# Matmuls that nobody reads, added to the tensor engine's program at both ends of an attention pipeline

## The chip, the cores and the metric

The kernel runs on one core of one Trainium2 chip. The metric is the device time of one execution in microseconds (us), from start to end. A "granted clock" of 1.00 in the profile means TensorE at 2.4 GHz, 0.50 means 1.2 GHz; a figure between them is the mean over a stretch in which both occurred.

## The reference: what is computed

The input is x of 8 x 512 rows of 512 numbers. Three residual blocks follow each other, each on the layer-normalised rows:

```python
x = x + 0.5 * ffn(layernorm(x))     # 16 experts choose 256 rows each; one shared 512x512 matrix
x = x + attention(layernorm(x))     # below
x = x + 0.5 * ffn(layernorm(x))
```

```python
q, k, v = x @ Wq, x @ Wk, x @ Wv                  # 16 heads, 4 shared k/v heads, q and k twice 32 wide
energy  = causal(rope(q) . rope(k))               # two maps for each head
scores  = softmax(energy / sqrt(32))
diff    = softmax(causal(scores[0] - lam * scores[1]))
att     = rmsnorm(diff @ v) @ Wo
```

## The kernel before

The program has three blocks. The first computes the expert layer, whose choice of rows is a search with small steps. The second, called the attention stage here, computes attention and, for each tile, the router logits and the expert product of the last block. The third makes the second choice and adds.

**Tiles.** The 4096 rows are 32 tiles of 128. Each matrix product with a weight is split into fp16 high and low parts (`three`, lines 229 to 235): 3 matmuls for each of 4 slices of the contraction, so 12 matmuls of 512 columns for a 512-wide result.

**The attention stage.** Every engine runs the same schedule, `run_bodies`. There are 33 bodies, K = 0 to 32, each of 8 steps (a step is one head for two of the four row tiles), each step of three slots; slot 3j+i is slot i of step j. On TensorE a step has the energies (`energies`, L1928 and L1930), the fp32 transposes of the difference (`turn_diff`, L1942), and the product with v (`weigh`, L1960, fp32, 33 columns). Beside these, a body does side work, given by a table from slot to functions:

- `prep(f)` works on tile tau = K + 5, the one that is to be projected: turn x (slot 1), three projections (slots 5, 7, 13), three groups of transposes (12, 19, 22). From K = 27 on there is no such tile, tau is `None`, and these slots are empty. PSUM bank 4 belongs to this work.
- `post(f)` works on tile pi = K - 5, the one that is to be finished: turn the heads (slot 7), the product with Wo (`product_o`, 10), turn x2 (17), route (20), expert (21). For K = 0 to 4 pi is `None`. PSUM bank 5 belongs to this work.

So bodies 0 to 4 have projections and nothing to finish (called the head bodies here), bodies 5 to 26 have both (the middle), bodies 27 to 31 only finish (the tail), and body 32 drains the steps that lag behind; its side table ends at slot 12. Before body 0 a prologue prepares tiles 0 to 4; after body 32 a closing finishes the last tiles. TensorE issues in program order, so whatever stands in a slot is done before the matmuls of the next slot. `energies(1)` waits until ScalarE has read the bank of the step before (`exp_done`); the bank 6 of the transposes is shared, and each use waits for ScalarE's `probs` (L1692).

**The order of the last block.** Nothing of the second choice starts before the closing has ended.

Of the kernel before, what the change touches and what calls it, by code (L numbers as in the profile page):

```python
# [31 lines left out]
KT = E // P  # L32
# [152 lines left out]
def program(nc, x, wqkv, wo, we, wr, lams, rms, rb, eb, consts, out, x1_d, x2_d, y2_d):  # L185
# [14 lines left out]
    with top:  # L200
# [709 lines left out]
        with ExitStack() as ctx:  # L910
# [994 lines left out]
            def _(pe):  # L1905
# [2 lines left out]
                    s.start(pe)  # L1908


                def energies(i):
                    def f(at):
                        j = at.j
# [51 lines left out]
                def prep(f):  # L1965
                    return lambda tau, pi: f(tau) if tau is not None else None

                def post(f):
                    return lambda tau, pi: f(pi) if pi is not None else None
# [84 lines left out]
                    tr.then_inc(rt_done.sem, 1)  # L2054

                def prologue():
                    first_turn(0)
                    for u in range(AHEAD):
                        first_project(u, 0)
                        if u >= 1:  # L2060
                            first_chunks(u - 1, 1)
                        first_project(u, 1)
                        if u >= 1:
                            first_chunks(u - 1, 2)
                        if u + 1 < AHEAD:
                            first_turn(u + 1)
                        first_project(u, 2)
                        first_chunks(u, 0)
                    first_chunks(AHEAD - 1, 1)
                    first_chunks(AHEAD - 1, 2)  # L2070
# [30 lines left out]
                def close_heads(q):  # L2101
                    al_done.wait(pe, LAST + q)
                    if q >= 2:
                        at_out.wait(pe, LAST + q - 2)
                    close_turn(c_pair(0, q), c_split(q), ant_done)
# [23 lines left out]
                def closing():  # L2129
# [2 lines left out]
                    expert(LAST - 1)  # L2132
                    prob_done.wait(pe, 2 * pair(NT - 1, STEPS - 1) + 1)
                    att_out.wait(pe, (NT // TB) * H - 1)
                    close_heads(0)
                    close_o(0)
                    close_heads(1)
# [13 lines left out]

                run_bodies(pe, [[(0, energies(1)), (0, energies(0)), (7, turn_diff(1))], [(8, weigh), (6, turn_diff(0))],
                                []],
                           {1: [prep(turn_x)], 5: [prep(project(0))], 7: [post(turn_heads), prep(project(1))],
                            10: [post(product_o)], 12: [prep(turn_chunks(0))], 13: [prep(project(2))],
                            17: [post(turn_x2)], 19: [prep(turn_chunks(1))], 20: [post(route)], 21: [post(expert)],
                            22: [prep(turn_chunks(2))]}, {},
                           prologue,
                           closing)
# [102 lines left out]
```

## Time and profile before

| | |
|---|---|
| time, median of 3 runs | 1826.18 us (1823.63 to 1830.19) |
| the profiled execution: its own time, its span | 1838.54 us, 1836.7 us |
| mean granted TensorE clock | 0.863 |
| busy share: TensorE, VectorE, ScalarE, GpSimdE | 80%, 79%, 69%, 59% |
| the attention stage's bodies with energies | from 288.0 us to 1663.2 us |

The span is the time from the first to the last instruction. A busy share is over the whole span and mixes stages. Matmuls are pipelined, so the duration of one is longer than the distance to the next; where a cost is worked out, the distance between two starts is used. The start of a body is taken as the start of its first energy matmul (L1928; 32 a body).

### The profile page before, as it was taken

Reading aid. Unit: us, or ns where it says so; the run is one execution under the profiler, and the core shown is the slowest. Engines: PE = TensorE matmul, PEld = TensorE weight load, DVE = VectorE, ACT = ScalarE, POOL = GpSimd, SP = SyncE. Lnnn points to the kernel's source line nnn. Section 1 sums busy time; section 2 is a strip of 40 time slices with the busy share of each in tenths; the row PEclk is TensorE's granted clock in tenths of the full one; section 3 lists DMA queues with packets and bytes.
Section 4 is the critical chain, followed back from the end, with each engine's and each line's share of the span. In section 5 each row is a group of like instructions: output and inputs, shape, how many; then the busy total and the mean of one; then the engine's idle time right before and its main releaser. Section 6 shows DMA issues by size and latency. Waiting matters only on the chain. (4 is left out here: it accounts for less than half of the span.)

```text
span 1836.7 us, 43825 instructions
## 1 busy us (share of the span) xinstructions
PE 1473.0 (80%) x10688; PEld 1035.1 (56%) x10688; DVE 1456.8 (79%) x5505; ACT 1260.1 (69%) x3426; POOL 1082.6 (59%) x1493
## 2 busy tenths in 40 slices
PE   3997645888898998889888898888988888888620
PEld 3543322666666666666666666666666666666310
DVE  5778425888889898898889988898989877674477
ACT  2363334888788888888888888888888876675320
POOL 4421443666677677776777777777777665554300
PEclk9998776788899899999999899998999887676855
DMA  8023321111111111121111111121211100001186
GB/s 304 2 64 135 118 66 42 29 32 36 32 46 46 44 50 50 44 50 44 44 44 44 44 44 50 46 52 45 51 46 45 42 19 21 19 17 41 41 312 252
DMA packets 179673, 117.30 MB, mean 64 GB/s; under 512 B 139169, under 2 KB 139553, under 8 KB 179618
## 3 DMA queue, kind: packets, MB, share of 16 engines
q1 hardware_dynamic: 179618, 116.65, 21.5%
q8 instruction: 25, 0.41, 0.1%
q14 instruction: 30, 0.25, 0.0%
HBM read 51.57 MB, written 33.55 MB: 46 GB/s over the span
## 5 line engine op out<-in xcount | busy, mean ns | idle before, releaser
L1675 ACT ACTIVATE ex<-bank,nbias 128x512 f32<-128x512 f32 (+3 forms) x1024 | 527.7, 538 | 83.2 <-DVE bank L1220 80.6
L1220 DVE TENSOR_SCALAR_CACHE_REDUCE bank<-bank,nesc 128x512 f32<-128x512 f32 (+3 forms) x1024 | 503.3, 551 | 84.6 <-PE bank L1930 83.9
L1960 PEld LDWEIGHTS bank<-vs,pr 128*128 128x128 f32 x2560 | 336.3, 207 | 24.5 <-issue 12.7
L1960 PE MATMUL bank<-vs,pr 128*128 (+1 forms) x2560 | 341.4, 284 | 9.8 <-DVE att L1266 5.3
L1942 PE MATMUL bank<-cst,df 128*128 128x128 f32 x1280 | 265.9, 310 | 83.6 <-ACT pr L1692 83.0
L1928 PE MATMUL bank<-ks,qs 96*128 (+2 forms) x1024 | 266.2, 337 | 68.7 <-ACT ex L1675 45.4
L1522 POOL TENSOR_SCALAR ex<-ex,gam 128x128 f32<-128x128 f32 (+3 forms) x512 | 317.3, 630 | 0.0
L1692 ACT ACTIVATE pr<-bank 128x128 f32<-128x128 f32 (+3 forms) x512 | 231.7, 453 | 88.5 <-PE bank L1942 87.3
L1246 DVE CUSTOM_DVE_ANT_0 df<-ex 128x128 f32<-128x128 f32 (+3 forms) x512 | 261.1, 525 | 8.2 <-issue 3.7
L1942 PEld LDWEIGHTS bank<-cst,df 128*128 128x128 f32 x1280 | 169.8, 167 | 111.0 <-ACT pr L1692 96.2
L1675 ACT ACTIVATION_READ_ACCUMULATOR ex<-bank,nbias 128x1 f32 x1024 | 222.6, 217 | 0.0
L1930 PE MATMUL bank<-mask_b,ident_b 128*128 128x128 bf16 x1024 | 210.2, 239 | 0.0
L1684 ACT ACTIVATE df<-df,dbias,rsum 128x512 f32<-128x512 f32 (+1 forms) x256 | 201.7, 788 | 0.0
L1928 PEld LDWEIGHTS bank<-ks,qs 96*128 (+1 forms) x1024 | 110.8, 108 | 160.7 <-issue 96.1
L1529 POOL TENSOR_SCALAR df<-df,rsum,dbias 128x128 f32<-128x128 f32 (+1 forms) x256 | 147.1, 575 | 40.9 <-DVE dbias L1255 40.8
L1605 POOL TENSOR_TENSOR split<-rot,split 128x512 f16<-128x512 f32 (+1 forms) x81 | 80.4, 993 | 111.3 <-ACT split L1720 111.3
L232 PE MATMUL bank<-wqkv_h,b_xt 128*128 128x512 f16 x360 | 142.3, 395 | 3.2 <-ACT turned L1762 1.2
L234 PE MATMUL bank<-wqkv_h,b_xt 128*128 128x512 f16 x360 | 142.9, 397 | 0.0
L233 PE MATMUL bank<-wqkv_l,b_xt 128*128 128x512 f16 x360 | 142.2, 395 | 0.0
L1234 DVE SCALAR_TENSOR_TENSOR gam<-esum,lam,rsum 128x2 f32<-128x2 f32 x256 | 114.8, 449 | 33.7 <-DVE rsum L1227 24.5
L1220 DVE DVE_READ_ACCUMULATOR bank<-bank,nesc 128x1 f32 x1024 | 141.2, 138 | 0.0
L1515 POOL TENSOR_SCALAR_AFFINE_SELECT ex<-ex 128x256 f32<-128x256 f32 x256 | 120.9, 472 | 22.2 <-DVE gam L1234 22.2
(359 smaller groups left out, 2954.5 us busy)
## 6 DMA issues: line engine op xcount, KB each, us to landing
qs<-turned SPq DMA_DIRECT2D x360, 64.0 KB, 2.1
x_dram<-xa SPq DMA_DIRECT2D x8, 1024.0 KB, 4.9
c_x<-x_dram SPq DMA_DIRECT2D x8, 1024.0 KB, 14.7
c_y<-y_dram SPq DMA_DIRECT2D x8, 1024.0 KB, 14.7
out_dram<-c_x SPq DMA_DIRECT2D x8, 1024.0 KB, 4.7
b_xs<-x_dram SPq DMA_DIRECT2D x30, 256.0 KB, 2.7
xa<-in_x SPq DMA_DIRECT2D x7, 1024.0 KB, 13.6
x<-x_dram SPq DMA_DIRECT2D x28, 256.0 KB, 2.6
```

The lines of the kernel that those rows point to most:

```text
L234: mm = eng.matmul(acc, a_lo(k), b_hi(k), start=False, stop=last and k == KT - 1)
L1220: dve.tensor_scalar(part, part, nesc[:, 0:1], None, ALU.mult, ALU.min, accum_out=nbias[:, j, i, a:a + 1]).then_inc(bias_done.sem, 1)
L1246: dve.tensor_tensor_reduce(out=df[j % 4][:, lo:hi], in0=ex[j % 4][:, 0, lo:hi], in1=ex[j % 4][:, 1, lo:hi], scale=1.0, scalar=-3e38, op0=A ...
L1522: gp.tensor_scalar(ex[j % 4][:, 1, lo:hi], ex[j % 4][:, 1, lo:hi], gam[:, j, i:i + 1], 1.0, ALU.mult, ALU.mult).then_inc(scaled.sem, 1)
L1529: gp.tensor_scalar(df[j % 4][:, lo:hi], df[j % 4][:, lo:hi], rsum[:, j, 0, 0:1], dbias[:, j, 0:1], ALU.mult, ALU.add).then_inc(shifted_sho ...
L1675: ac.activation(ex[j % 4][:, a, lo:hi], energy(j, i)[:, a, :], ACT.Exp, bias=nbias[:, j, i, a:a + 1], scale=-1.0, accum_out=esum[:, j, i, ...
L1684: ac.activation(df[j % 4][:, lo:hi], df[j % 4][:, lo:hi], ACT.Identity, bias=dbias[:, j, 1:2], scale=rsum[:, j, 1, 0:1]).then_inc(shifted_ ...
L1692: ac.activation(pr[j % 2][:, lo:hi], bank[:, 6, 0:hi - lo], ACT.Exp).then_inc(prob_done.sem, 1)
L1928: pe.matmul(out_e, q.rearrange("p a n -> p (a n)"), k.rearrange("p a n -> p (a n)"), start=True, stop=True)
L1930: mm = pe.matmul(out_e[:, n - P:n], ident_b[:, :], mask_b[:, :], start=False, stop=True, skip_group_check=True)
L1942: tr = pe.transpose(bank[:, 6, k * P:(k + 1) * P], df[j % 4][:, lo + k * P:lo + (k + 1) * P], ident)
L1960: mm = pe.matmul(bank[:, 7, t * DV:(t + 1) * DV], pr[j % 2][:, lo + k * P:lo + (k + 1) * P], val, start=(k == 0), stop=(k == t))
```

## The change

A helper `busy(n, at)` issues n matmuls of 128 x 128 weights (the fp16 identity) and 512 fp16 columns (a slice of the expert matrix) into PSUM bank `at`. Nobody reads the result, and no semaphore is raised. `idle_prep(n)` calls it in bodies in which tau is `None`, into bank 4; `idle_post(n)` in bodies in which pi is `None`, into bank 5. Twelve more are put ahead of the first transposes of the prologue, behind a new wait for the first normalised tile (`xn_done`), and twelve into the closing, between the last waits and `close_heads(0)`.

Counted: 28 in each of the bodies 27 to 31 (slots 2, 5, 7, 10, 13, 18 and 21, four each), 16 in body 32 (slots 2, 5, 7, 10), 12 in each of the bodies 0 to 4 (slots 11, 16, 20), 12 in the prologue, 12 in the closing: 240 in all.

```diff
+                def busy(n, at):
+
+                    for i in range(n):
+                        pe.matmul(bank[:, at, :], ident_h[:, :], we_h[:, i % KT, :], start=True, stop=True)
+
+                def idle_prep(n):
+                    return lambda tau, pi: busy(n, 4) if tau is None else None
+
+                def idle_post(n):
+                    return lambda tau, pi: busy(n, 5) if pi is None else None
...
                 def prologue():
+                    xn_done.wait(pe, 0)
+                    busy(12, 0)
                     first_turn(0)
...
                     att_out.wait(pe, (NT // TB) * H - 1)
+                    busy(12, 4)
                     close_heads(0)
...
-                           {1: [prep(turn_x)], 5: [prep(project(0))], 7: [post(turn_heads), prep(project(1))],
-                            10: [post(product_o)], 12: [prep(turn_chunks(0))], 13: [prep(project(2))],
-                            17: [post(turn_x2)], 19: [prep(turn_chunks(1))], 20: [post(route)], 21: [post(expert)],
+                           {1: [prep(turn_x)], 2: [idle_prep(4)], 5: [idle_prep(4), prep(project(0))], 7: [idle_prep(4), post(turn_heads), prep(project(1))],
+                            10: [idle_prep(4), post(product_o)], 12: [prep(turn_chunks(0))], 11: [idle_post(4)], 13: [idle_prep(4), prep(project(2))],
+                            16: [idle_post(4)], 17: [post(turn_x2)], 19: [prep(turn_chunks(1))], 18: [idle_prep(4)], 20: [idle_post(4), post(route)], 21: [idle_prep(4), post(expert)],
                             22: [prep(turn_chunks(2))]}, {},
```

## Rows read from the trace of the kernel before

**Rows 1.** The page, busy tenths and granted clock in 40 slices of the span.

```profile
PE   3997645888898998889888898888988888888620
DVE  5778425888889898898889988898989877674477
PEclk9998776788899899999999899998999887676855
```

**Rows 2.** Busy time by stretch, bodies 6 to 8; columns: stretch, length, engines, clock, DMA.

```profile
535.59:577.07 41.48, 36.85 (x305) 26.89 (x303) 38.86 (x154) 35.89 (x102) 31.24 (x44) 1.00 0.19 49
577.07:623.10 46.03, 41.28 (x305) 29.09 (x302) 39.71 (x154) 36.78 (x103) 34.62 (x51) 0.89 0.17 44
623.10:665.64 42.54, 38.05 (x305) 27.92 (x302) 39.13 (x154) 36.38 (x102) 30.55 (x42) 0.96 0.18 48
```

**Rows 3.** The same view, the five tail bodies, K = 27 to 31.

```profile
1453.83:1494.29 40.46, 35.18 (x241) 27.48 (x239) 31.15 (x134) 31.87 (x94) 24.52 (x37) 0.79 0.18 45
1494.29:1535.11 40.82, 35.08 (x240) 27.44 (x238) 31.47 (x134) 31.54 (x93) 24.49 (x37) 0.79 0.06 19
1535.11:1581.71 46.60, 41.22 (x239) 30.58 (x237) 31.28 (x134) 31.88 (x93) 24.61 (x37) 0.67 0.05 17
1581.71:1626.24 44.53, 39.91 (x240) 30.18 (x238) 31.26 (x134) 31.66 (x93) 24.53 (x37) 0.69 0.06 18
1626.24:1663.16 36.92, 32.12 (x208) 25.29 (x206) 28.66 (x120) 27.75 (x83) 21.47 (x32) 0.72 0.06 21
```

**Rows 4.** The same view, head bodies K = 0, 1 and 3.

```profile
288.01:324.67 36.66, 24.83 (x135) 13.69 (x136) 28.68 (x116) 23.80 (x75) 17.67 (x26) 0.69 0.16 35
324.67:366.49 41.82, 37.99 (x248) 29.12 (x249) 33.93 (x144) 33.12 (x99) 26.09 (x42) 0.79 0.14 32
407.91:449.10 41.19, 34.98 (x248) 26.00 (x249) 34.14 (x145) 33.11 (x99) 25.94 (x41) 0.88 0.13 30
```

**Rows 5.** The same view, short stretches in body 29, in the drain and before the closing.

```profile
1531.60:1545.10 13.50, 10.45 (x81) 7.54 (x78) 8.98 (x41) 10.79 (x34) 7.04 (x8) 1.00 0.05 19
1545.20:1558.60 13.40, 13.38 (x56) 9.25 (x57) 7.73 (x33) 8.26 (x24) 9.28 (x15) 0.50 0.00 0
1671.40:1688.50 17.10, 14.62 (x63) 10.52 (x62) 5.16 (x17) 6.15 (x11) 8.92 (x9) 0.50 0.08 26
1695.30:1712.30 17.00, 8.42 (x43) 4.38 (x43) 7.26 (x18) 4.33 (x7) 13.39 (x5) 0.50 0.00 1
```

**Rows 6.** TensorE's instructions in order of time, body 28 and 29; columns: start, duration.

```profile
1532.10 0.38 PE L233 MATMUL bank<-we_l,at 128*128 128x512 f16 x1
1532.31 0.38 PE L234 MATMUL bank<-we_h,at 128*128 128x512 f16 x1
...
1553.88 0.63 PE L233 MATMUL bank<-wo_l,at 128*128 128x512 f16 x1
1554.30 0.63 PE L234 MATMUL bank<-wo_h,at 128*128 128x512 f16 x1
...
1558.57 0.48 PE L1928 MATMUL bank<-ks,qs 96*128 x1
```

**Rows 7.** TensorE's waits in the tail bodies : total us, times, longest; the largest.

```profile
PE bank L1928 <- ACT ex L1675: 21.9, 16, 2.3
```

**Rows 8.** Order of time at the prologue: VectorE, TensorE, and SyncE's stacking DMAs.

```profile
196.17 0.55 DVE L1306 TENSOR_SCALAR b_xs<-b_xs,norms 128x512 f32<-128x512 f32 x1 [0.67 <-POOL norms L1551]
...
198.71 1.03 PE L2027 MATMUL bank<-ident_h,att 128*128 128x128 f16 x8 [25.39 <-POOL att L1555]
...
200.85 0.61 PE L232 MATMUL bank<-wqkv_h,b_xt 128*128 128x512 f16 x1 [1.10 <-ACT b_xt L1777]
...
219.24 8.41 SPq L1123 DMA_DIRECT2D qs<-turned  x12
```

**Rows 9.** TensorE in order of time at the closing.

```profile
1712.08 0.75 PE L2098 MATMUL bank<-ident_h,qs 128*128 128x128 f16 x8
1713.94 0.39 PE L232 MATMUL bank<-wo_h,qs 128*128 128x512 f16 x1 [1.10 <-ACT qs L1853]
```

## The prediction

> **What bounds the kernel now.** I read the page's slices first, then the busy times cut at the starts of bodies, then order of time and waits where the clock moves. In the page the reader is to see two dips of the granted clock that lie inside the attention stage: the head bodies and, deeper, the tail (the digits 7, 6, 7, 6 of the clock under an 8 or 9 of TensorE) [rows 1]. The last dip, to 5, is the second choice, which runs on VectorE; the change does not touch it.
>
> In the middle three engines are close: at full clock body 6 takes 41.48 us with TensorE busy 36.85 and VectorE 38.86, that is 89% and 94% [rows 2]. There the clock alone changes the length: 42.54 us at 0.96, 46.03 at 0.89. A clock of c over a body of length l holds 2(1 - c)l of time at 1.2 GHz, called cold time below. For body 7 that is 10.1 us, and it is 4.55 us longer than body 6: 0.45 us for each cold us.
>
> The tail is where one sees something odd [rows 3]. VectorE has 31 us of work a body instead of 39, ScalarE 32 instead of 36, TensorE some 240 matmuls instead of 305, and yet the bodies take 40.5 to 46.6 us. TensorE is the engine that fills them, 87% to 90% busy, because it is slow: the clocks of 0.79, 0.79, 0.67, 0.69 and 0.72 are 17.0, 17.1, 30.8, 27.6 and 20.7 us of cold time, 113 of 209.3 us. From body 28 to 29 the length rises by 5.78 us for 13.7 cold us: 0.42. I take 0.43 us for each cold us.
>
> What precedes a fall or a rise? In body 29 the clock is full for 13.5 us, in which TensorE is busy 10.45, falls after that, and stays at 1.2 GHz for 13.4 us in which it is busy 13.38 [rows 5]. So busy time by itself does not bring the clock back. It comes back behind the twelve 512-column matmuls of the product with Wo: those start 0.43 us apart, and the energies at 1558.57 already speed up [rows 6]. At full clock they start 0.21 to 0.22 us apart. Dense 512-column matmuls are the ingredient that the tail has lost with its projections (36 of them a body), and are what the change adds (28 a body).
>
> The Trainium skill (TensorE: Matmul & The Clock Gate, Part 1) says that sustained activity releases the throttle and that idle gaps bring it back. Taken literally it speaks against the change: TensorE is busy throughout the cold stretch [rows 5], so more matmuls would add only their own time. The same page, Part 4, says that transposes do not count as busy in the same way; the tail's steps consist largely of fp32 transposes and of 33-column products, and with that the trace agrees.
>
> **The change, term by term.** *Tail, bodies 27 to 31.* First, what a warm tail would be without additions: 40.46 - 17.0 x 0.43 = 33.1, and likewise 33.5, 33.4 and 32.7 us for the next three, which agree, and 28.0 for the shorter last one. At 33.2 us VectorE's 31.3 would be 94%, the share it reaches in body 6, so this is also a floor.
>
> Now the additions: 28 x 0.216 = 6.0 us of TensorE a body. Its busy time of 35.18 us shrinks by half of the cold time to 26.7, and grows to 32.7. At the 89% that TensorE reaches in body 6, a body takes 36.8 us at full clock. That is dearer than 33.2: in this form the additions hide only partly. What can hide them is TensorE's wait for ScalarE before the energies, 21.9 us in 16 places of the five bodies, none over 2.3 us [rows 7]; the groups of four (0.86 us) stand mostly right before energies. Those in slots 10 and 21 stand ahead of a product or an expert, where TensorE is behind anyway, and are exposed. At 1.2 GHz a group costs 1.7 us and nothing hides it.
>
> How much cold time remains is the disputed number. The middle, whose 36 dense matmuls come in three lumps, has 0, 10.1 and 3.4 us in its three bodies [rows 2], 4.5 on average; the additions are spread over seven places and ought to do as well. I take 4.5 us, 1.9 us of length. The four bodies are then 38.7 us each. Body 31, with 24 of the additions ahead of its last energies, is (32.12 - 10.3 + 5.2) / 0.89 + 1.9 = 32.2. Sum 187.0 against 209.3: **-22.3 us**. Bounds: full clock throughout, 177.5, so -31.8; the clock of today throughout, which is a rival below.
>
> *Drain, body 32.* Cold from 1671.4 to 1688.5 [rows 5]. Its end would be 7.4 us earlier without that; I take half, 3.7, and half of the 16 x 0.216 = 3.5 us exposed: **-2.0**, between -7 and +5.
>
> *Closing.* The twelve come where TensorE follows the expert's product without a pause, and ScalarE waits for the transposes behind them (1.10 us from its copy back to TensorE) [rows 9]. The clock is up from 1712.3 on, before it has work there, so nothing is gained: 12 x 0.216 = **+2.6**; at 1.2 GHz it would be 5.1. No cover: the last block waits for the closing's end.
>
> *Prologue.* The added wait ends with the first normalised tile, at 196.7; TensorE then would have waited until 198.71 for the low part [rows 8]. Twelve cold matmuls end at 201.8, 3.1 us late. In exchange the clock rises earlier, and about six of the first projection's matmuls, today at 0.43 us, cost 0.21 less each: **+1.8**, between 0 and 3.1. Everything behind follows, since SyncE's queue of stacking DMAs starts from that projection's results at 219.24 and is what body 0 waits for.
>
> *Head, bodies 0 to 4.* Here length hardly follows the clock: body 1 has 17.6 cold us and 41.82 us, body 3 has 9.9 and 41.19 [rows 4], 0.08 per cold us. So little is to be won, and 12 x 0.216 = 2.6 us find 6.2 us of idle TensorE in body 3. Nothing for bodies 1 to 4, **-1** for the start in body 0 (22.7 cold us); between -4 and +6. The middle is unchanged but meets the clock in another phase: 0, plus or minus 3.
>
> Sum: -22.3 - 2.0 + 2.6 + 1.8 - 1 = -20.9, from 1838.5 to 1817.6 for the profiled execution. The median of the timed runs is 12.4 us lower than that. Bodies 29 and 30 together are 9.9 us longer than 27 and 28 for the same work; if that is what the timed executions lack, only 11 us are to be won there. I go halfway: -16 from 1826.2, **1810 us**.
>
> **Rivals.** *The clock stays* (slower). If the additions do not change when it falls and rises, the 136 in the five bodies cost about 0.33 us each at today's mix, 45 us, of which the 21.9 us of waits can swallow half their own length or all of it: +23 to +34; with drain +5, closing +2.6 and prologue +3.1 the time is about 1860 to 1871. For it: the long busy cold stretch, and that a group of four is a third of what stood before the rise in body 29. Against it: the middle, where as dense a mixture holds 0.89 to 1.00. *The point from which this decides*: exposed additions are between 136 x 0.216 - 16 x 0.86 = 15.6 and 29.4 us at full clock, so the cold time must fall by 36 to 68 of 113 us, that is, the tail's clock must reach 0.82 to 0.89. *Bought even*: the clock reaches about 0.85, gain and price cancel, and only closing and prologue remain: 1822 to 1832. *Slower by the head*: the same place in the projections' chain (slot 11 ahead of the transposes of chunk 0) could delay rope and stacking by up to its 0.86 us a body, +6 at most with the others; this alone moves the result but does not turn it.
>
> **How the numbers follow.** The tail clocks over 0.89: 0.60, giving 1793 to 1819. Bought even: 0.17. The clock stays or rises little, and the time is above 1832: 0.23. A measurement of this kernel tells 0.3%, 5.5 us, from no change; so faster 0.62, same 0.15, slower 0.23. Low end: the full-clock tail against the timed median, 1826.2 - 31.8 + 2.6 + 1.8 - 1 = 1797.8, and some 4 for the drain: 1794. High end: into the slower rival, whose mild form, a clock of 0.80, gives some +10: 1836. The likeliest case alone spans 1794 to 1820.
>
> **What would show it.** Right: tail clocks of 0.9 and more, bodies of 37 to 40 us, TensorE still near 88% busy, waits for ScalarE before energies fewer than 16; head bodies still 41 to 42 us; close_heads 2.6 us later behind the expert, the first projection 2 us later. Wrong: tail clocks near 0.8 with bodies of 43 us or more; or full clocks and bodies of 40 us, which would mean that the 6 us are exposed on top of VectorE's floor, not beside it.

## The result and the profile after

In the session of the recorded result the changed kernel is slower, by under one per cent: median 1843.56 us (19 runs, 1829.54 to 1852.55) against 1826.77 us of the kernel before (19 runs, 1823.31 to 1854.24). The ratio is 1.0075, with a 95% interval of 1.005 to 1.01. The forecast was 1810 us and "faster"; the time lies above the range's 1836. The profiled execution took 1848.64 us, with a span of 1846.8 us. Ratios and intervals here and below leave out the few runs that lie more than 1.5% above the fastest of their kernel; medians and counts keep them.

The times of the changed kernel fall into two groups: over all sessions of this study none of its 31 runs lies between 1837.3 and 1843.4 us, 19 lie below (median 1833.2) and 12 above (1849.2), and 11 of those 12 belong to the 19 runs of the first session. The kernel before has no such gap. Its 94 runs crowd at 1822 to 1830 and thin out up to 1860; cut at the same 1840, a line drawn after the fact, 70 lie below (1826.7) and 24 above (1849.3). So two things have to be explained: some 6.5 us, or 0.36%, between the lower groups, and how often a run lies far above.

The slices of the page, kernel after, of 46 us each. They answer to [rows 1]:

```profile
PE   3996735999999989898998888999998988887720
...
PEclk9998877778899998999999999999999899998865
```

The dip of the tail (7, 6, 7, 6 before) has become 9, 9, 9, 8: the clock did what the change is made for. The digits of the head are what they were, and that is the first disappointment.

The windows between the first energies of successive bodies, kernel after: start and end, length, then the busy time and count of TensorE, its weight loads, VectorE, ScalarE and GpSimd, the granted clock, the DMA share and GB/s. The order is bodies 0, 1, 3 and 4, a body of the middle, all of bodies 5 to 26, the tail's bodies 27 to 31, and from the last energies to the closing transposes. They answer to [rows 2 to 4]:

```profile
286.11:320.76 34.65, 23.57 (x147) 12.84 (x148) 28.59 (x116) 23.81 (x75) 17.68 (x26) 0.84 0.17 37
320.76:364.81 44.05, 40.18 (x260) 28.98 (x261) 33.94 (x144) 33.12 (x99) 26.09 (x42) 0.81 0.13 30
...
408.99:453.25 44.26, 40.39 (x261) 29.05 (x261) 33.91 (x145) 33.12 (x99) 26.01 (x41) 0.81 0.13 28
453.25:494.26 41.01, 37.15 (x260) 27.14 (x261) 34.13 (x145) 33.13 (x99) 25.95 (x41) 0.88 0.14 30
...
984.90:1029.28 44.38, 39.78 (x305) 28.09 (x303) 38.92 (x154) 36.38 (x102) 31.96 (x45) 0.92 0.18 46
...
494.26:1473.54 979.28, 881.00 (x6623) 624.73 (x6624) 855.51 (x3368) 800.58 (x2246) 706.87 (x995) 0.92 0.18 45
...
1473.54:1515.18 41.64, 37.20 (x268) 26.54 (x266) 31.08 (x134) 31.98 (x94) 24.59 (x37) 0.92 0.18 44
1515.18:1554.40 39.22, 34.11 (x268) 24.20 (x266) 31.32 (x134) 31.45 (x93) 24.59 (x37) 1.00 0.06 20
1554.40:1594.38 39.98, 35.38 (x268) 25.01 (x266) 31.36 (x134) 31.55 (x93) 24.51 (x37) 0.96 0.06 20
1594.38:1634.84 40.46, 36.55 (x268) 26.13 (x266) 31.22 (x134) 31.56 (x93) 24.21 (x37) 0.92 0.06 19
1634.84:1668.44 33.60, 28.51 (x233) 20.58 (x230) 28.71 (x121) 27.55 (x83) 22.22 (x33) 1.00 0.07 23
...
1668.44:1722.37 53.93, 40.47 (x232) 27.84 (x231) 19.52 (x63) 19.67 (x41) 26.55 (x21) 0.75 0.09 30
```

The same windows of the kernel before that [rows 2 to 4] don't have, all of bodies 5 to 26 and the stretch behind the last energies:

```profile
490.20:1453.83 963.63, 864.80 (x6622) 623.76 (x6623) 862.28 (x3368) 800.75 (x2246) 712.64 (x995) 0.93 0.18 46
...
1663.16:1712.08 48.92, 35.81 (x199) 25.38 (x198) 19.61 (x65) 19.66 (x41) 27.18 (x22) 0.65 0.10 33
```

Span against span, 1836.7 to 1846.8, the 10.1 us are made up like this:

| stretch | before | after | difference |
|---|---|---|---|
| start to first energies | 288.0 | 286.1 | -1.9 |
| body 0 | 36.7 | 34.7 | -2.0 |
| bodies 1 to 4 | 165.5 | 173.5 | +8.0 |
| bodies 5 to 26, not touched | 963.6 | 979.3 | +15.7 |
| bodies 27 to 31 | 209.3 | 194.9 | -14.4 |
| last energies to closing transposes | 48.9 | 53.9 | +5.0 |
| the rest | 124.6 | 124.4 | -0.2 |

The largest term is in bodies in which nothing was added: there nearly every body takes 44.4 us, where before their average was 963.6 / 22 = 43.8.

In the waits of TensorE over bodies 27 to 31, kernel after (total us, times, longest), the first row answers to [rows 7]:

```profile
PE bank L1939 <- ACT ex L1675: 13.5, 17, 1.4
...
PE bank L1953 <- ACT pr L1692: 5.0, 14, 0.6
```

The waits before the energies, 21.9 us in 16 places before, became 13.5 us in 17. The second row is a wait for ScalarE at the transposes of the difference; the kernel before had 1.5 us of it in 5 places. So the waits for ScalarE shrank by about 5 us in all, and the additions are 29.4 us of matmuls (136 x 0.216).

The order of time on TensorE at both ends, kernel after (start, duration, line, tiles, and in brackets the wait before it); it answers to [rows 8, 9]:

```profile
193.96 4.45 PE L1914 MATMUL bank<-we_h,ident_h 128*128 128x512 f16 x12 [23.45 <-DVE b_xs L1306]
198.24 0.61 PE L2038 MATMUL bank<-ident_h,att 128*128 128x128 f16 x8
199.96 0.39 PE L232 MATMUL bank<-wqkv_h,b_xt 128*128 128x512 f16 x1 [1.10 <-ACT b_xt L1777]
...
1719.77 2.75 PE L1914 MATMUL bank<-we_h,ident_h 128*128 128x512 f16 x12
1722.37 0.61 PE L2111 MATMUL bank<-ident_h,qs 128*128 128x128 f16 x8
```

Behind the expert the twelve take 2.60 us from their start to that of the closing transposes.

### The profile page after: what moved, and what is told of

It is laid out like the page before. It is cut to its first block and busy times, and to the rows that moved or that the text cites. A ratio compares the mean times of both kernels' runs of the same rounds, so it can differ in the third digit from the quotient of the medians.

```text
span 1846.8 us, 44305 instructions
## 1 busy us (share of the span) xinstructions
PE 1495.6 (81%) x10928; PEld 1025.7 (56%) x10928; DVE 1448.8 (78%) x5505; ACT 1259.3 (68%) x3426; POOL 1076.8 (58%) x1493
## 5 line engine op out<-in xcount | busy, mean ns | idle before, releaser
L1971 PEld LDWEIGHTS bank<-vs,pr 128*128 128x128 f32 x2560 | 322.2, 199 | 26.8 <-issue 14.4
L1971 PE MATMUL bank<-vs,pr 128*128 (+1 forms) x2560 | 326.9, 278 | 12.3 <-DVE att L1266 7.4
L1953 PE MATMUL bank<-cst,df 128*128 128x128 f32 x1280 | 257.4, 303 | 88.3 <-ACT pr L1692 87.6
L1522 POOL TENSOR_SCALAR ex<-ex,gam 128x128 f32<-128x128 f32 (+3 forms) x512 | 313.5, 623 | 0.0
L1939 PE MATMUL bank<-ks,qs 96*128 (+2 forms) x1024 | 254.6, 325 | 52.9 <-ACT ex L1675 29.7
L1246 DVE CUSTOM_DVE_ANT_0 df<-ex 128x128 f32<-128x128 f32 (+3 forms) x512 | 256.6, 516 | 9.2 <-issue 4.7
L1675 ACT ACTIVATION_READ_ACCUMULATOR ex<-bank,nbias 128x1 f32 x1024 | 227.9, 223 | 0.0
L1953 PEld LDWEIGHTS bank<-cst,df 128*128 128x128 f32 x1280 | 162.5, 161 | 116.5 <-ACT pr L1692 102.4
L1941 PE MATMUL bank<-mask_b,ident_b 128*128 128x128 bf16 x1024 | 203.1, 233 | 0.0
L1684 ACT ACTIVATE df<-df,dbias,rsum 128x512 f32<-128x512 f32 (+1 forms) x256 | 202.4, 791 | 0.0
L232 PE MATMUL bank<-wqkv_h,b_xt 128*128 128x512 f16 x360 | 138.9, 386 | 3.2 <-ACT turned L1762 1.2
L234 PE MATMUL bank<-wqkv_h,b_xt 128*128 128x512 f16 x360 | 138.1, 384 | 0.0
```

What stands on the lines that cost most here:

```text
L232: eng.matmul(acc, a_hi(k), b_hi(k), start=first and k == 0, stop=False)
L1246: dve.tensor_tensor_reduce(out=df[j % 4][:, lo:hi], in0=ex[j % 4][:, 0, lo:hi], in1=ex[j % 4][:, 1, lo:hi], scale=1.0, scalar=-3e38, op0=A ...
L1522: gp.tensor_scalar(ex[j % 4][:, 1, lo:hi], ex[j % 4][:, 1, lo:hi], gam[:, j, i:i + 1], 1.0, ALU.mult, ALU.mult).then_inc(scaled.sem, 1)
L1675: ac.activation(ex[j % 4][:, a, lo:hi], energy(j, i)[:, a, :], ACT.Exp, bias=nbias[:, j, i, a:a + 1], scale=-1.0, accum_out=esum[:, j, i, ...
L1684: ac.activation(df[j % 4][:, lo:hi], df[j % 4][:, lo:hi], ACT.Identity, bias=dbias[:, j, 1:2], scale=rsum[:, j, 1, 0:1]).then_inc(shifted_ ...
L1939: pe.matmul(out_e, q.rearrange("p a n -> p (a n)"), k.rearrange("p a n -> p (a n)"), start=True, stop=True)
```

## The experiments

Every kernel below computes all that the reference asks for; where an edit is called "nothing of the change", the additions are other ones than the change's. Each was timed in five rounds, beside the kernel before on the same chip. Lengths of bodies are windows as above, from one profiled execution of each kernel. Each diff is against the kernel that it varies: the changed kernel for the three parts, tail_only for tail_lean, the kernel before for middle_fill, middle_fill for middle_three, and middle_three for middle_thin and combined. The sessions' medians of the kernel before are 1829.32 (first four experiments, 35 runs), 1832.75 (next four, 23) and 1834.57 (last four, 17).

### The change in three parts

**tail_only**, the additions in bodies 27 to 31 alone.

```diff
 def idle_prep(n):
-    return lambda tau, pi: busy(n, 4) if tau is None else None
+    return lambda tau, pi: busy(n, 4) if tau is None and not isinstance(pi, int) else None
...
 def prologue():
-    xn_done.wait(pe, 0)
-    busy(12, 0)
...
-    busy(12, 4)
     close_heads(0)
...
-    ... 11: [idle_post(4)], ... 16: [idle_post(4)], ... 20: [idle_post(4), post(route)] ...
+    ... 20: [post(route)] ...
```

> Only the 28 added matmuls in each of the bodies 27 to 31; nothing in the head, the prologue, the drain, the closing. Theory A (the tail's additions pay, the loss lies elsewhere): the tail takes 195 us instead of 209, as in the changed kernel; the timed runs that leave the middle at 43.7 us a body are 4 to 14 us faster than those of before. Theory B (the tail's additions cost what they bring): no gain, and any tail shorter than 209 us in the profile is already given back in the drain.

Measured: median 1823.65 us (12 runs, 1819.22 to 1840.24), ratio 0.9977, interval 0.994 to 1.0013. The tail takes 197.0 us. Two of its windows:

```profile
1451.40:1490.64 39.24, 34.26 (x267) 24.24 (x266) 31.17 (x134) 31.76 (x94) 24.60 (x37) 1.00 0.18 47
1490.64:1533.10 42.46, 39.38 (x266) 28.41 (x265) 31.32 (x134) 32.07 (x93) 24.22 (x37) 0.84 0.05 19
```

Alternate bodies hold the full clock all through, as the theory wants, and even those are no shorter than 39.2 us. Where the clock falls for part of a body, it takes 42.5. The middle takes 960.1 us, as it does in ends_only, tail_double and tail_half: tail additions alone do not disturb it. (The 963.6 us of the kernel before come mostly from its last middle body, 44.1 us instead of 40.9.)

**head_only**, the additions of slots 11, 16 and 20 in bodies 0 to 4 alone (slots 2, 5, 7, 10, 13, 18 and 21 and both ends taken out).

```diff
-    2: [idle_prep(4)], 5: [idle_prep(4), prep(project(0))], ...
+    5: [prep(project(0))], 7: [post(turn_heads), prep(project(1))], 10: [post(product_o)], 11: [idle_post(4)], ...
```

> Only the 12 added matmuls in each of the bodies 0 to 4. Theory A: they slow bodies 1 to 3 from 41.4 to 44.2 us as in the changed kernel, 8 us, of which body 0 gives back 2; the time is 5 to 8 us above before. Rival (those long head bodies were a chance meeting of schedule and clock, not the additions' price): head bodies of 41 to 42 us, no change beyond 3 us.

Measured: median 1833.83 us (12 runs, 1829.53 to 1852.68), ratio 1.0037, interval 1.0002 to 1.0073. Body 0, body 2, body 3, and the first part of body 2 and of body 3:

```profile
289.06:324.20 35.14, 24.06 (x148) 12.96 (x148) 28.61 (x116) 23.82 (x75) 17.68 (x26) 0.84 0.17 37
...
368.56:412.81 44.25, 40.39 (x260) 29.06 (x261) 33.86 (x144) 33.05 (x99) 25.95 (x41) 0.81 0.12 28
412.81:453.81 41.00, 37.13 (x261) 27.10 (x261) 34.15 (x145) 33.13 (x99) 25.95 (x41) 0.88 0.13 30
...
368.56:382.20 13.64, 13.64 (x63) 10.19 (x64) 8.14 (x37) 9.84 (x29) 8.72 (x15) 0.50 0.29 61
...
412.90:419.70 6.80, 6.80 (x39) 5.58 (x40) 5.05 (x22) 5.86 (x17) 6.22 (x11) 0.50 0.26 56
```

Body 2 begins with 13.64 us at a clock of 0.50, that is at 1.2 GHz throughout, with TensorE busy for all of it; body 3 does so for 6.80 us. That is the difference between 44.25 and 41.00 us. Where the cold stretch is short, the additions are free: 41.0 is what such a body took before [rows 4]. Body 0 gains some 1.5 us. The head costs more than it gives.

The additions do not themselves stand in the cold stretch. In body 2 they start at 390.42, 401.87 and 406.15 us, and the granted clock around each is 1.00; from 368.56 to 382.20 TensorE runs only what the kernel before has there too. And the long cold stretch is not theirs alone. Of seven profiles in which bodies 1 to 4 have no additions, six show four bodies of 41.1 to 41.9 us, and one, that of tail_lean below, shows 39.7 us and then three of 44.2 to 44.4. The three profiles with additions there show three, two and two bodies of 44.0 to 44.4 us.

**ends_only**, the twelve ahead of the first turn and the twelve ahead of close_heads alone (all of the slots' additions taken out).

```diff
-    2: [idle_prep(4)], 5: [idle_prep(4), prep(project(0))], ... 11: [idle_post(4)], ...
+    5: [prep(project(0))], 7: [post(turn_heads), prep(project(1))], ...
```

> Only the twelve matmuls in the prologue and the twelve in the closing. Theory A: closing +2.6 us, prologue 0 to +2, nothing gained: +2 to +5 us, and the middle may fall into its other pattern (44.37 us a body instead of 43.69), which would add 14 us more in some runs. Rival (the prologue's additions warm the clock for what follows): body 0 shorter by 2 us or more and no loss in all.

Measured: median 1831.81 us (12 runs, 1824.72 to 1850.88), ratio 1.003, interval 0.9985 to 1.0075. Its tail has no additions, so it is also a second look at the tail of the kernel before, the first four bodies:

```profile
1447.38:1487.93 40.55, 34.98 (x239) 27.47 (x238) 31.12 (x134) 31.87 (x94) 24.51 (x37) 0.79 0.17 45
1487.93:1528.78 40.85, 34.88 (x239) 27.43 (x238) 31.46 (x134) 31.54 (x93) 24.49 (x37) 0.79 0.05 19
1528.78:1570.26 41.48, 35.44 (x239) 27.77 (x238) 31.45 (x134) 31.77 (x93) 24.56 (x37) 0.79 0.06 19
1570.26:1610.80 40.54, 34.78 (x239) 27.41 (x238) 31.27 (x134) 31.55 (x93) 24.50 (x37) 0.79 0.06 19
```

None is like bodies 29 and 30 of [rows 3], with 46.60 and 44.53 us at 0.67 and 0.69. The tail takes 198.5 us (198.2 in head_only, 199.4 in middle_fill, 198.7 on average), not 209.3. A good 10 us of what there was to win was a mishap of the one profiled execution.

Below 1840 us the medians of the three parts are 1822.85, 1833.5 and 1830.15, against 1826.7 of the kernel before: -3.9, +6.8 and +3.4. They sum to +6.3, and the lower group of the changed kernel lies +6.5 higher. That they agree to 0.2 us is luck: against the runs of the kernel before in their own session (1825.7) the parts are -2.8, +7.9 and +4.5, in sum +9.5, and each rests on 8 to 11 runs that spread over 9 to 19 us. What holds is the order: the tail gains 3 to 4 us, the head loses 7 to 8, the ends 3 to 5.

### What the tail's bodies are bound by

**tail_lean**, tail alone, 20 a body instead of 28: none in slots 2, 10 and 21, eight in slot 13.

```diff
-    2: [idle_prep(4)], ... 10: [idle_prep(4), post(product_o)], ... 13: [idle_prep(4), prep(project(2))], ... 21: [idle_prep(4), post(expert)]
+    10: [post(product_o)], ... 13: [idle_prep(8), prep(project(2))], ... 21: [post(expert)]
```

> Only the tail, 20 added matmuls a body instead of 28, at the places behind which the clock fell in the tail without additions (slots 5, 7, 13, 18; eight in slot 13, where TensorE still waited 1.4 us with four); nothing in slots 2, 10 and 21. If the price of an addition is its own time wherever TensorE does not wait, the three dropped groups give back up to 2.6 us a body: 37 to 38 us at full clock instead of 39.2, 8 to 12 us in all against before. If the length of a warm tail body is not set by TensorE, it stays 39 us and the time stays that of the tail alone.

Measured: median 1811.22 us (6 runs, 1806.02 to 1836.27), ratio 0.9888, interval 0.9827 to 0.995. The profiled execution is the longest of the six, 1836.27 us, so its lengths are not those of a typical run. Its tail takes 190.4 us; two of its windows:

```profile
1470.57:1508.69 38.12, 35.17 (x259) 25.80 (x258) 31.00 (x134) 31.57 (x94) 24.62 (x37) 0.91 0.19 48
...
1589.16:1627.43 38.27, 33.82 (x258) 24.28 (x257) 31.39 (x134) 31.59 (x93) 24.58 (x37) 0.96 0.07 21
```

At a clock of 0.91 such a body is shorter than one with 28 additions at full clock (39.24 in tail_only). So some of the groups in slots 2, 10 and 21 are paid for; which ones is shown step by step below.

Where the excess of this execution lies can be read too. Bodies 1 to 4 and bodies 5 to 26, none of which this kernel changes:

```profile
325.49:498.08 172.59, 147.58 (x993) 107.81 (x994) 135.92 (x573) 132.45 (x390) 104.35 (x162) 0.84 0.13 29
498.08:1470.57 972.49, 872.27 (x6600) 628.01 (x6623) 860.23 (x3368) 802.31 (x2246) 714.86 (x995) 0.92 0.18 46
```

They are 7 and 12 us longer than the usual 165.5 and 960.1. Long executions thus exist without any addition outside the tail, and the head has a part in them.

**tail_double**, tail alone, every group 8 instead of 4, so 56 a body (`idle_prep(8)` in each of the seven slots).

> Only the tail, groups of eight instead of four (56 a body). If additions are paid in full at full clock: 39.2 + 6.0 = 45.2 us a body and +25 us or more against the tail alone. If they are half hidden, as my prediction had it: 42 us and +13 us.

Measured: median 1828.37 us (12 runs, 1823.69 to 1850.27), ratio 1.0005, interval 0.9963 to 1.0046. The tail takes 200.3 us. A body at full clock:

```profile
1492.08:1533.16 41.08, 39.18 (x295) 26.92 (x293) 31.24 (x134) 31.41 (x93) 24.21 (x37) 1.00 0.06 19
```

28 more additions are 28 x 0.216 = 6.0 us of matmuls; the body grows from 39.2 to 41.1 us. Two thirds went into time in which TensorE would have waited. So at 39.2 us TensorE was not the bound, and at 41.1, busy 39.18, it nearly is.

**tail_half**, tail alone, groups of 2, so 14 a body (`idle_prep(2)` in each of the seven slots).

> Only the tail, groups of two in all seven slots (14 a body). With 28 a body a full-clock body took 39.2 us, with 56 it took 41.1: 1.9 us for 6.0 us of matmuls. If that line goes on, a full-clock body with 14 takes 38.3 us; if an unadded warm body is as short as my prediction had it (33.2 us), it takes 36 us. With only 14 the clock will fall once or twice a body, so the tail as a whole takes 194 to 200 us.

Measured: median 1832.86 us (12 runs, 1826.43 to 1850.56), ratio 1.0001, interval 0.9961 to 1.0041. The tail takes 202.4 us, some 4 more than with none. The worst body:

```profile
1489.39:1533.44 44.05, 39.71 (x253) 29.48 (x252) 31.48 (x134) 31.71 (x93) 24.18 (x38) 0.77 0.05 18
```

No body holds the full clock (0.77 to 0.87, against 0.78 and 0.79 with none), and the tail is longer than the 194 to 200 us expected. Too small a dose buys nothing; that it is worse than none is seen in one profile and not in the times, whose ratio is 1.0001.

### The middle, which the change leaves alone

**middle_fill**, nothing of the change; four matmuls in slot 18 of bodies 5 to 26.

```diff
+def mid_fill(n):
+    def f(tau, pi):
+        if tau is None or pi is None:
+            return
+        rope_v.wait(pe, 3 * tau + 2)
+        v_done.wait(pe, tau)
+        busy(n, 4)
+    return f
...
-    17: [post(turn_x2)], 19: ...
+    17: [post(turn_x2)], 18: [mid_fill(4)], 19: ...
```

> Nothing of the change; instead four 512-column matmuls into bank 4 in slot 18 of bodies 5 to 26, where the clock of the changed kernel's middle falls once a body (0.92). Theory A (a middle body's length is set by where its clock falls, and dense matmuls at that place keep it up): clock 1.0 and 41.5 to 42.5 us a body, 25 to 45 us faster in all. Rival (added matmuls cost their time in full, as they did in the tail): 0.9 us more a body against at most 2.9 us won, or a fall at another place: within 10 us of before.

Measured: median 1825.6 us (12 runs, 1823.67 to 1834.68), ratio 0.9972, interval 0.9937 to 1.0006. A body:

```profile
798.70:840.46 41.76, 37.47 (x308) 27.28 (x306) 39.33 (x154) 36.15 (x103) 32.04 (x45) 1.00 0.19 49
```

One group a body changes the pattern and not its mean (the middle takes 962.8 us, against 960.1 without). But none of the 12 runs lies above 1840, where 24 of 94 of the kernel before do.

**middle_three**, nothing of the change; slot 18 as in middle_fill, and two more groups placed inside waits of TensorE: one ahead of the turned heads, in the middle and the tail, and one ahead of the product with v in step 4, in every body from 1 on. So a middle body has 12, a tail body 8 and a head body from 1 on 4.

```diff
 def turn_heads(u):
     y_out.wait(pe, u - 1)
+    busy(4, 5)
     al_done.wait(pe, u)
...
     if j % 2 == 0:
         att_out.wait(pe, at.heads(j // 2 - 1))
+    if j == 4:
+        busy(4, 7)
```

> Nothing of the change; groups of four at the three places of a middle body behind which the clock still fell with one group: before the heads are turned (slot 7, where TensorE waits 1.2 us for GpSimdE), before the product with v in step 4 (1.5 us of wait behind it; this one in every body from 1 on) and in slot 18. If a middle body's length is set by its cold time and additions into waits are free: clock 1.0, 41.5 to 42.5 us a body, 25 to 45 us faster in all. If additions are paid in full: 43 to 44 us a body at a clock near 1.0, within 8 us of before. Either way no runs near 1850, since there is no second pattern to fall into.

Measured: median 1792.92 us (6 runs, 1788.39 to 1796.0), ratio 0.9782, interval 0.9726 to 0.9838. The middle takes 929.3 us; its first body takes 45.7 us and the next 41.8, all others are like this one:

```profile
618.26:660.35 42.09, 39.12 (x315) 28.04 (x314) 39.66 (x154) 36.18 (x103) 32.36 (x46) 1.00 0.19 48
```

The clock stays full, and the middle is 34.3 us shorter than in the profile before (963.6), 31 us shorter than the usual 960.1. The additions lengthen such a body by no more than 0.6 us: body 6 of the kernel before took 41.48 us at full clock without additions [rows 2].

**middle_thin**, middle_three with each group of four replaced by eight fp32 matmuls of 33 columns.

```diff
-    for i in range(n):
-        pe.matmul(bank[:, at, :], ident_h[:, :], we_h[:, i % KT, :], start=True, stop=True)
+    for i in range(2 * n):
+        pe.matmul(bank[:, at, 0:DV], ident, cst[:, 0:DV], start=True, stop=True)
```

> As the middle with three places, but each group of four 512-column fp16 matmuls is replaced by eight 33-column fp32 matmuls, which keep TensorE busy for the same 0.9 us (0.11 us each at full clock). If busy time keeps the clock up: 42.1 us a body and 1793 us again. If dense streaming does: the clock falls as before, 43.7 to 44.5 us a body, 1825 to 1845 us.

Measured: median 1880.0 us (6 runs, 1878.99 to 1884.11), ratio 1.0238, interval 1.0184 to 1.0292. That is above both times that were expected. They were meant to keep TensorE busy for the same time; the trace shows them busy for nearly twice as long. Two groups at full clock, middle_three's and then middle_thin's, where the profiler records each fp32 matmul as two:

```profile
714.16 1.03 PE L1914 MATMUL bank<-we_h,ident_h 128*128 128x512 f16 x4
...
742.16 1.87 PE L1914 MATMUL bank<-cst 128*128 128x33 f32 x16
```

Two bodies of the middle:

```profile
683.13:730.55 47.42, 45.81 (x352) 34.71 (x350) 39.46 (x154) 37.02 (x103) 35.09 (x51) 0.89 0.16 43
730.55:772.95 42.40, 41.16 (x351) 31.84 (x350) 39.02 (x154) 36.47 (x102) 29.51 (x41) 1.00 0.19 48
```

Where the clock is full, the body takes 42.40 us, little more than middle_three's. But the clock falls, with TensorE busy for 97% of each of these bodies. Over the whole middle it is 0.95, against 0.99 in middle_three and 0.93 in the kernel before, and the middle takes 980.6 us. In the same places the dense groups kept the clock up and the thin ones did not, although they were busy for longer. Columns and number type changed together, so which of the two decides is not shown. The 87 us between the two kernels are not the clock's alone: 51 lie in the middle, 17 in bodies 1 to 4 and 17 in the tail. In the tail neither kind does much for the clock: 0.74 to 0.84 with the thin groups, 0.75 to 0.83 with the dense ones.

### The changed kernel again, and the best version

**changed_again**, the changed kernel itself.

> The changed kernel once more. Its times lie in two groups, 1830 to 1836 and 1843 to 1853, with granted clocks of 0.890 to 0.894 and 0.884 to 0.889. If the middle's pattern makes the groups, a profile of a time in the lower group shows 43.7 us a middle body on average and one in the upper group 44.4, and the head and tail the same in both. If the head or the tail makes them, the middle is the same in both.

Measured: median 1832.89 us (12 runs, 1825.61 to 1846.91), ratio 1.0012, interval 0.9976 to 1.0047. Its profiled execution took 1829.87 us and shows the lower group: a body of the head, all of bodies 5 to 26, and two of them.

```profile
322.23:366.38 44.15, 40.28 (x261) 29.01 (x261) 33.95 (x144) 33.14 (x99) 26.09 (x42) 0.81 0.13 30
...
492.50:1455.90 963.40, 862.73 (x6599) 623.76 (x6622) 860.70 (x3367) 800.81 (x2247) 712.60 (x996) 0.93 0.18 46
...
670.99:712.46 41.47, 36.80 (x304) 26.87 (x303) 38.86 (x154) 35.88 (x102) 31.23 (x44) 1.00 0.19 49
712.46:758.49 46.03, 41.06 (x303) 29.11 (x302) 39.70 (x154) 36.79 (x103) 34.63 (x51) 0.89 0.17 44
```

The middle takes 963.4 us in the pattern of the kernel before (41.47, 46.03 and 42.54 again, with 44.2 twice between), where the first profile of the same kernel had 979.3 us and 44.4 in every body. The two executions differ by 18.8 us, and 15.9 of them lie there. Another 3.1 lie in bodies 1 to 4 (170.4 instead of 173.5 us), of which two instead of three take 44 us; the tail takes 197.0 us instead of 194.9.

**combined**, middle_three with three groups more in the tail, in slots 5, 13 and 18, so 20 matmuls in a tail body.

```diff
+    5: [idle_prep(4), prep(project(0))], ... 13: [idle_prep(4), prep(project(2))], ... 18: [idle_prep(4), mid_fill(4)], ...
```

> Nothing in the head's slots, the prologue, the drain's own slots or the closing; the three groups of four in the middle as in the run with three places, and in the tail groups in slots 5, 13 and 18 beside the one before the turned heads and the one before the product with v in step 4. If both gains add: middle 42.1 us a body, tail 38 to 39 instead of 40.8 a body, 1780 to 1786 us. If the tail only looks shorter and gives it back in the drain: 1790 to 1793.

Measured: median 1775.91 us (6 runs, 1772.54 to 1782.9), ratio 0.9681, interval 0.9627 to 0.9735. The middle takes 927.6 us, with bodies as in middle_three, and the tail 182.8. A body of the tail:

```profile
1449.38:1486.88 37.50, 32.54 (x258) 23.50 (x257) 31.33 (x134) 31.48 (x93) 24.59 (x37) 1.00 0.06 21
```

and the waits of TensorE for ScalarE before the energies in that tail body:

```profile
PE bank L1948 <- ACT ex L1675: 2.8, 5, 0.8
```

With 20 well placed additions a tail body at full clock takes 37.50 us. TensorE is busy 87% of it, ScalarE and VectorE 84%: none is full, and the five waits together are 2.8 us, none over 0.8.

**combined_of_3**, the same with groups of 3.

> The same with groups of three. If the middle's 42.1 us at full clock against 41.5 without additions is the additions' price, it falls to about 41.9 as long as the clock stays up, 3 us less in all; if three are too few at one place, some bodies show a clock of 0.92 to 0.96 and take 42.5 to 44 us, 10 us or more slower.

Measured: median 1779.24 us (6 runs, 1775.66 to 1785.05), ratio 0.9701, interval 0.9648 to 0.9753. The middle takes 927.3 us and its bodies 42.1 at full clock, so 0.6 us less of additions do not shorten them. The tail takes 188.4 at clocks of 0.90 to 0.96, 5.6 us more than with groups of 4.

### A tail body step by step

The same windows cut at the first energies of the eight steps of a body (four matmuls of L1928 or its like in each) show where a cold us and where an addition is paid for. Length in us and granted clock; body 28 of ends_only is an ordinary body without additions, body 29 of the kernel before the odd one of [rows 3], and in the last two columns the clock is 1.00 throughout:

| step | ordinary, none | odd, none | combined, 20 | tail_only, 28 |
|---|---|---|---|---|
| 0 | 3.39 at 1.00 | 3.39 at 1.00 | 3.39 | 3.52 (slot 2) |
| 1 | 4.38 at 1.00 | 4.37 at 1.00 | 4.38 (slot 5) | 4.26 (slot 5) |
| 2 | 5.78 at 0.68 | 5.78 at 0.69 | 5.42 (slot 7) | 5.40 (slot 7) |
| 3 | 6.63 at 0.76 | 9.92 at 0.50 | 5.46 | 6.33 (slot 10) |
| 4 | 4.73 at 1.00 | 4.78 at 0.86 | 4.74 (two groups) | 4.73 (slot 13) |
| 5 | 4.36 at 0.74 | 5.63 at 0.50 | 4.25 | 4.25 |
| 6 | 4.73 at 0.50 | 4.74 at 0.50 | 4.51 (slot 18) | 4.50 (slot 18) |
| 7 | 6.85 at 0.77 | 7.99 at 0.65 | 5.35 | 6.22 (slot 21) |
| body | 40.85 | 46.60 | 37.50 | 39.21 |

The rows behind the readings: steps 3 and 6 of the ordinary body, steps 3 and 7 of combined and of tail_only, and step 6 at full clock without a group in slot 18 (middle_thin, body 28).

```profile
1501.48:1508.11 6.63, 6.63 (x39) 4.74 (x38) 4.53 (x20) 5.29 (x15) 5.80 (x11) 0.76 0.00 0
1517.20:1521.93 4.73, 4.73 (x36) 4.11 (x35) 3.29 (x15) 4.73 (x16) 3.77 (x9) 0.50 0.00 0
...
1462.57:1468.03 5.46, 5.29 (x39) 3.60 (x37) 4.74 (x21) 5.46 (x17) 5.17 (x10) 1.00 0.00 0
1481.53:1486.88 5.35, 5.30 (x36) 3.70 (x38) 2.85 (x15) 4.53 (x16) 2.98 (x6) 1.00 0.00 0
...
1546.28:1552.61 6.33, 6.16 (x44) 3.98 (x41) 4.76 (x21) 5.56 (x17) 6.04 (x12) 1.00 0.00 0
1566.09:1572.31 6.22, 6.17 (x41) 4.09 (x43) 2.87 (x15) 4.53 (x16) 2.99 (x6) 1.00 0.00 0
...
1562.04:1566.54 4.50, 3.15 (x34) 2.52 (x35) 4.08 (x18) 4.50 (x14) 4.19 (x9) 1.00 0.00 0
```

*What an addition costs.* The groups in slots 10 and 21 are paid in full: 6.33 against 5.46 and 6.22 against 5.35, 0.87 us each, which is the whole of 4 x 0.216. They are the 1.7 us between 37.50 and 39.21. The groups in slots 2, 5 and 13 cost nothing: steps 0 and 1 take 7.77 us without additions and 7.78 with two groups, step 4 takes 4.73 with none, one or two.

*What a cold us costs.* It depends on the step. In step 3, all of it at 1.2 GHz, 9.92 instead of 5.46 us is 0.45 for each cold us; in step 6, also all of it at 1.2 GHz, 4.73 instead of 4.50 is 0.05. The odd body has most of its additional cold time where it is dear: steps 3, 5 and 7 are 3.3, 1.3 and 1.1 us longer than in the ordinary one.

*A full-clock tail body without additions* stands in no trace, but most of its steps do: steps 0, 1 and 4 above, step 6 in the last row, and step 7, which took 5.36 us at a clock of 1.00 in body 29 of ends_only (1564.90 to 1570.26). Of combined's groups only the one in slot 7 can thus be exposed, with 0.86 us at most. So I estimate 36.6 to 37.5 us.

## Why the prediction was wrong

The forecast and what came of it, in us. The profile column compares the first profiles of the two kernels; the last column compares medians of the runs below 1840, part by part:

| term | forecast | profile | medians |
|---|---|---|---|
| bodies 27 to 31 | -22.3 | -14.4 | -3.9 (tail_only) |
| drain | -2.0 | +2.4 | |
| closing and prologue | +2.6 and +1.8 | +2.6 and +0.9 | +3.4 (ends_only) |
| bodies 0 to 4 | -1 | +6.0 | +6.8 (head_only) |
| middle | 0 | +15.7 | |

**What bounds it: right in kind.** The tail's clock rose with the added matmuls, from between 0.67 and 0.79 to between 0.92 and 1.00 (0.84 and 1.00 in tail_only and changed_again). The prediction took from [rows 5, 6] that busy time is not what brings it back. middle_thin against middle_three bears it out: the same places, nearly twice the busy time in the thin groups, and a clock of 0.95 instead of 0.99 over the middle, with TensorE 97% busy. The rule of the Trainium skill (TensorE: Matmul & The Clock Gate, Part 1) that sustained activity releases the throttle therefore does not hold here if activity is read as time busy.

**Remaining cold time: right in one profile of three.** 4.5 us a body were assumed. By 2(1 - c)l the first four bodies after have 6.7, 0, 3.2 and 6.5 us, 4.1 on average. In tail_only and changed_again they have 0, 13.6, 0 and 13.6, 6.8 on average.

**The step that failed: the tail's term, -22.3 us, and in it what cold time is worth.** Three sizes were wrong.

*The start, 209.3 us.* It is 10.6 us above an ordinary tail (198.7), whose bodies take 40.85 us and not 46.60. The prediction's "I go halfway" doubted this, and the doubt was right and half of it too little: none of the three other profiles of an unchanged tail has the excess. The tail's gain is 14.4 us from profile to profile and 1.7 to 3.8 against an ordinary tail.

*"0.43 us for each cold us", and with it a warm body of 33.2 us.* The slope came from body 7 of the middle and from bodies 28 and 29 of the odd tail, whose further cold time lay mostly in its dearest step. In an ordinary body 17 cold us cost 40.85 less 36.6 to 37.5, that is 0.20 to 0.25 each. The agreement of the four values near 33 proved nothing, since all were worked out with the same slope. VectorE's 94% "as a floor" was borrowed from the middle; at 37.50 us VectorE and ScalarE are 84% busy. What sets these 37.5 us, a chain through several engines with many short waits, I did not resolve.

*The full-clock body of the sum, 32.7 / 0.89 = 36.8 us.* Measured 39.2. The share was nearly right: TensorE is busy 34.26 of 39.24 us, 87%. The busy time was not: without the additions it is 34.26 - 6.0 = 28.2 us at full clock, and the prediction had 26.7, by taking off half of the cold time. That is 1.6 of the 2.4 us.

**The price of the additions: not too low but too high.** The prediction named slots 10 and 21 as exposed, and they are, with 0.87 us each. It priced all 28 at 36.8 - 33.2 = 3.6 us a body and took 15.6 us as the least that the five bodies could have exposed. Measured are 1.7 us a body, or 2.6 if the group in slot 7 is exposed too. The additions were cheaper than forecast and the full clock was worth less, and so the outcome in the tail is close to "bought even", though by another way: the clock went far over the 0.85 of that rival. The bodies of 39.2 us at full clock are the sign that the prediction itself gave for being wrong, but not for its reason: not 6 us of additions are exposed on top of VectorE's floor, the floor itself lies higher.

**Head: "Nothing for bodies 1 to 4", wrong by 8.** The slope of 0.08 per cold us in [rows 4] holds as long as the pattern of the clock does. With the additions the stretch at 1.2 GHz at the start of a body lasts 13.6 instead of 7 us in two or three of the four bodies; +8.0 us in the first profile, +5 in the two others, against a bound of +6 for the whole head. This is the rival "slower by the head", but not by its mechanism: the additions themselves run at full clock and cost nothing there. Why the cold stretch lasts longer stays open, all the more since one kernel without additions in the head shows it as well. Body 0 gained 2.0 where 1 was forecast.

**Ends: about right.** Closing +2.6, as predicted (1719.77 to 1722.37). Prologue: twelve matmuls from 193.96 to 198.24, then the projections at full clock. From the normalised tile to the first energies it is 92.8 us after and 91.8 before, +0.9 within the forecast 0 to 3.1 (tail_only, without it, has 92.5, so it may be less). The tile was ready 2.8 us sooner than before, ahead of any addition, and so the first energies come 1.9 us earlier all the same. Drain: 53.93 - 48.92 - 2.6 = +2.4 in one profile and 50.6 - 48.9 - 2.6 = -0.9 in changed_again; forecast -2.0, between -7 and +5.

**Middle: "0, plus or minus 3", wrong by 15.7 in the profile, right in the lower group.** The prediction saw that the middle meets the clock in another phase, and took the size from nothing. The loop has two patterns: a cycle of five bodies with a mean near 43.7 us, and 44.4 us in every body. The changed kernel was profiled in either; the kernel before was profiled once, in the first, so what its runs above 1840 do is not shown. The profile of tail_lean has stretches of both. The recorded ratio of 1.0075 is thus some 0.36% of additions plus long executions, 11 of 19 in that session. In a later session it was 1 of 12, with a ratio of 1.0012. Whether the additions make the costlier pattern likelier stays open: the kernel before has 24 of 94, and sessions differ. Of the 30 runs with dense groups in the middle itself (middle_fill, middle_three, combined, combined_of_3) none lies more than 10 us above its kernel's median.

The sum by measured terms, in the lower group: tail -3.9, head +6.8, ends +3.4, so +6.3 us on 1826.7, against 1833.2 measured; by the session's own runs of the kernel before the sum is +9.5. Of the 33 us between the forecast of 1810 and the median of 1843.56 some 10 are the long executions of that session; the rest is the tail above all, then the head.

## What to carry over

In this kernel matmuls that nobody reads were worth their time where they were dense (512 columns, fp16), stood in waits that TensorE has anyway, and came often enough that the clock stayed up for whole bodies; 14 a body in the tail were too few, and groups in exposed places (slots 10 and 21) cost their full time. Look for them where the most iterations are: the same idea in the 22 bodies of the middle gave 31 to 34 us, in the tail at best 16. And read a body's length in several profiles of kernels that don't differ there before pricing it, and cut it into its steps: a cold us cost 0.45 us in one step and 0.05 in another, and a slope drawn from one odd pair of bodies was the main error in the tail.

## What the runs showed of the hardware

- TensorE was busy 13.64 of 13.64 us at 1.2 GHz (head_only, 368.56 to 382.20) without its clock rising in that time; with 97% busy over whole bodies the clock averaged 0.89 to 1.00 (middle_thin).
- One program, unchanged, ran its 22 middle bodies in 963.4 or in 979.3 us, in two repeating patterns of body length and clock, the costlier with body after body of 44.37 or 44.38 us. Its 31 times lie in two groups, around 1833 and 1849 us.
- The same 1.2 GHz costs very different amounts: a step of the tail took 9.92 us at 0.50 and 5.46 at 1.00, another 4.73 at 0.50 and 4.50 at 1.00.
- More additions did not give steadily more: in one profile each, the tail took 202.4, 197.0 and 200.3 us with 14, 28 and 56 a body, 198.7 with none, and 182.8 with 20 in better places.
- A group of four 512-column matmuls (0.86 us at full clock) lengthened its step by 0.87 us in slots 10 and 21 and by nothing in slots 2, 5 and 13.
